# DeepFM forward pass on one core: later weight loads wait for the first gathered rows, the last tile's layer 1 outputs go by quarters, and the results are turned by VectorE in 32x32 blocks

## The chip, the core and the metric

The kernel runs on 1 core of one Trainium2 chip. The metric is the device time of one execution in microseconds (us). Three runs of the kernel before gave 155.88, 156.05 and 154.91 us, with a median of 155.88. One further execution was taken with the hardware profiler on. It took 154.75 us, of which its trace covers a span of 153.0 us.

## The reference

For 512 samples with 13 numeric and 26 categorical features the kernel computes a linear term, a factorization-machine term and a three-layer network, and adds them:

```
lin = bias + x_num @ w_num + lin_cat[fid, x_cat].sum(axis=1)
vn = x_num[:, :, None] * v_num[None, :, :]
vc = v_cat[fid, x_cat]                      # 26 rows of 64 numbers for each sample
v = concatenate([vn, vc], axis=1)
interactions = 0.5 * (v.sum(1)**2 - (v*v).sum(1)).sum(axis=1, keepdims=True)
deep_in = concatenate([x_num, vc.reshape(512, -1)], axis=1)      # 13 + 1664 columns
h = relu(deep_in @ W1 + b1)                 # 1024
h = relu(h @ W2 + b2)                       # 512
h = relu(h @ W3 + b3)                       # 256
return lin + interactions + h @ Wo + bo     # [512, 1]
```

All of it is in float32. The table holds 26 x 12500 rows of 65 numbers, the 64 of `v_cat` and the one of `lin_cat`.

## The kernel before

**Tiles and chunks.** The 512 samples are 4 tiles of 128 (one sample per partition, `t` = 0 to 3, `LAST` = 3). The 1664 gathered columns of a tile are 13 chunks of 128 columns (`c` = 0 to 12), two table rows each. So each chunk needs two indirect gathers, 26 for a tile and 104 in all. GpSimd (POOL) issues them in one row (lines 214 to 228). The buffer `g` holds 13 chunks, one tile: a gather for chunk `c` of the next tile waits until TensorE has turned that chunk, and until its squares and sums are done. `rows_in[c]` counts the gathers that have landed.

**Precision.** TensorE multiplies in fp32r. Each operand is therefore split in a high and a low part, and each product is three matmuls: high by high (L583), high by low weight (L590), low by high weight (L593). ScalarE makes high parts by a copy with rounding (`high_part`, `x_high`), VectorE makes low parts by a subtraction (`low_part`, `x_low`). For a weight's low part TensorE first copies the high part to PSUM (`twin`, L566).

**Weights.** 18 items of 128 x 1024 floats (512 KB each: 13 for W1, 4 for W2, 1 for W3) pass through a ring of 4 raw buffers. The loads are issued by SyncE (SP), in the order of lines 185 to 196; from the fifth on, each waits until the low part of the item four before is made (`lo_made`). In the same queue stand the categorical indices (`cat`), four copies of the numeric block (`hidden`, from which ScalarE and VectorE make `num_r` and the numeric terms), and `consts`.

**The order on TensorE is written out by hand.** A `step(t, c)` is `layer1_a` (L583), `turn_rows` of the next chunk (the transpose L574, which waits for that chunk's rows), and `layer1_b` (L590, L593). In tile 0 a `twin` stands before each step. Layers 2 and 3 of tile t-1 stand between the first steps of tile t. Engines run their instructions in order, so a wait in `turn_rows` holds all that follows it on TensorE.

**The results.** `interactions` (VectorE) gives `fm[:, t]`, `deep_sum` gives `deep[:, t]`, one number per partition. `result_row` (L700 to L706) turns both by a matmul against `ident` into one row of PSUM (two matmuls that add up), and VectorE copies that row to `out_row` (L449 to L451). For tiles 0 to 2 this stands inside a step of a later tile; for tile 3 it is the end of the program, followed by a store of 512 B.

**The last tile's end.** `layer1_last(3)` ends each half of layer 1 in its own PSUM bank. Then come relu by halves (L267 on ScalarE, L412 on VectorE), eight transposes of 128 columns (`turn_hidden1`, L642), high and low parts by halves (L271, L416), and layer 2 in two halves of 256 outputs (L792, L793, L798), then layer 3.

## Time and profile before

| | |
|---|---|
| three runs, median | 155.88 us (154.91 to 156.05) |
| profiled execution | 154.75 us |
| its span in the trace | 153.0 us |
| TensorE (PE) busy | 135.2 us, 88% of the span |
| GpSimd (POOL) busy | 99.6 us, 65% |
| VectorE (DVE) busy | 77.7 us, 51% |
| ScalarE (ACT) busy | 58.0 us, 38% |
| granted TensorE clock | 1.00 |

Each time is of one profiled execution. An engine's busy share is an average over the whole span: what an engine is worth at a certain place is read from what waits for it there. "issue" is time in which an engine waited for nothing that the profile shows. Line numbers (L225) are those of the kernel before.

### The profile page before, as it was taken

The page shows a single profiled execution, that of the slowest core. Times are in us where ns is not written, and L with a number is a line of the kernel's source. Part 1 is how long each engine was busy: PE and PEld are TensorE (multiplying, and loading weights), DVE is VectorE, ACT ScalarE, POOL GpSimd, SP SyncE. Part 2 cuts the span into 40 slices and gives each one's busy share as a digit, 9 for nine tenths or more (in the row PEclk, how much of TensorE's full clock was granted, in tenths as well). Part 3 has the DMA queues.
Part 4 walks back from the last instruction along what each step waited for, and adds up shares of the span by engine and source line. Part 5 has one row for each costly group of instructions (what it writes and reads, how often), then busy time and mean ns, then how long its engine had stood idle before and what let it go on. Part 6 is the DMA issues. An engine that isn't in the chain of part 4 may idle for free.

```text
span 153.0 us, 2072 instructions
## 1 busy us (share of the span) xinstructions
PE 135.2 (88%) x661; PEld 105.0 (69%) x661; DVE 77.7 (51%) x216; ACT 58.0 (38%) x153; POOL 99.6 (65%) x111
## 2 busy tenths in 40 slices
PE   0303999879999999999999999999999999999994
PEld 0102776547776676888767878778787887776992
DVE  4310587997699687232435524333446223353712
ACT  4501578666376631142333132223431423234120
POOL 3777777777777777777777777777777777700000
PEclk9999999999999999999999999999999999999999
DMA  4999677987777643343234343431344433310000
GB/s 107 372 123 311 103 208 197 298 261 198 192 232 201 175 27 29 28 29 25 27 25 33 26 26 28 27 31 27 25 30 27 30 28 25 28 9 4 0 0 0
DMA packets 6750, 13.66 MB, mean 89 GB/s; under 512 B 2578, under 2 KB 2708, under 8 KB 6740
## 3 DMA queue, kind: packets, MB, share of 16 engines
q0 software_dynamic: 3328, 3.47, 25.6%
q1 hardware_dynamic: 3412, 10.07, 21.0%
q8 instruction: 5, 0.08, 0.2%
q14 instruction: 5, 0.04, 0.1%
HBM read 13.53 MB, written 0.00 MB: 88 GB/s over the span
## 4 chain that ended last, share of the span: by engine, by line
PE 67%; DVE 13%; DMA 12%; issue 3%; ACT 2%; POOL 1%; DVEq 0%
PE acc L593 12%; PE acc L590 12%; PE acc L583 11%; DMA raw<-in_weights 6%; DMA g<-in_table,rows 6%; DVE w_lo L371 4%; PE acc L659 4%; PE acc L655 3%; PE acc L656 3%; PE xt_ps L574 3%; PE acc L677 2%; DVE num_r L376 1%; ACT w_hi L234 1%; DVE hidden L412 1%; PE ht_ps L566 1%
## 5 line engine op out<-in xcount | busy, mean ns | idle before, releaser
L225 POOL DMA_INDIRECT g<-in_table,rows x104 | 98.8, 950 | 33.2 <-issue 28.3
L398 DVE TENSOR_TENSOR x_lo<-xt_ps,x_hi 128x128 fp32r<-128x128 f32 x52 | 15.0, 288 | 50.0 <-ACT x_hi L241 50.0
L241 ACT ACTIVATE x_hi<-xt_ps 128x128 fp32r<-128x128 f32 x52 | 14.3, 275 | 68.6 <-PE xt_ps L574 68.4
L590 PE MATMUL acc<-w_lo,x_hi 128*128 128x512 f32 x96 | 34.8, 443 | 0.0
L583 PE MATMUL acc<-w_hi,x_hi 128*128 128x512 f32 x96 | 31.1, 405 | 0.8 <-ACT x_hi L241 0.5
L593 PE MATMUL acc<-w_hi,x_lo 128*128 128x512 f32 x96 | 30.8, 402 | 1.0 <-DVE x_lo L398 1.0
L593 PEld LDWEIGHTS acc<-w_hi,x_lo 128*128 128x128 f32 x96 | 18.1, 191 | 6.0 <-DVE x_lo L398 1.8
L583 PEld LDWEIGHTS acc<-w_hi,x_hi 128*128 128x128 f32 x96 | 17.7, 191 | 5.4 <-ACT x_hi L241 1.4
L234 ACT ACTIVATE w_hi<-raw 128x1024 fp32r<-128x1024 f32 x18 | 19.0, 1055 | 6.2 <-DMA raw<-in_weights 6.1
L574 PE MATMUL xt_ps<-ident,g 128*128 128x128 f32 x52 | 14.4, 278 | 6.8 <-DMA g<-in_table,rows 6.8
L590 PEld LDWEIGHTS acc<-w_lo,x_hi 128*128 128x128 f32 x96 | 14.7, 193 | 4.9 <-issue 0.9
L371 DVE TENSOR_TENSOR w_lo<-raw,ht_ps 128x512 fp32r<-128x512 f32 x24 | 15.8, 680 | 2.6 <-PE ht_ps L566 2.6
L404 DVE TENSOR_REDUCE field_sum<-g 128x64 f32<-128x256 f32 (+1 forms) x28 | 15.8, 563 | 0.0
L566 PE MATMUL ht_ps<-w_hi,ident_r 128*128 128x512 f32 x24 | 9.4, 433 | 6.1 <-ACT w_hi L234 6.1
L574 PEld LDWEIGHTS xt_ps<-ident,g 128*128 128x128 f32 x52 | 7.5, 144 | 9.9 <-DMA g<-in_table,rows 7.5
L251 ACT ACTIVATE junk_sq<-g 128x256 bf16<-128x256 f32 (+1 forms) x28 | 11.0, 393 | 0.1
L566 PEld LDWEIGHTS ht_ps<-w_hi,ident_r 128*128 128x128 f32 x24 | 5.0, 211 | 7.0 <-issue 6.1
L655 PE MATMUL acc<-w_hi,h1t_hi 128*128 128x512 f32 x24 | 9.6, 401 | 0.0
L656 PE MATMUL acc<-w_lo,h1t_hi 128*128 128x512 f32 x24 | 9.5, 396 | 0.0
L371 DVE TENSOR_TENSOR w_lo<-raw,acc 128x512 fp32r<-128x512 f32 x12 | 8.2, 680 | 2.4 <-PE acc L566 2.3
L659 PE MATMUL acc<-w_hi,h1t_lo 128*128 128x512 f32 x24 | 6.7, 400 | 0.1
L416 DVE TENSOR_TENSOR h1t_lo<-ht_ps,h1t_hi 128x512 fp32r<-128x512 f32 x8 | 5.4, 689 | 1.7 <-ACT h1t_hi L271 1.4
(99 smaller groups left out, 154.4 us busy)
## 6 DMA issues: line engine op xcount, KB each, us to landing
raw<-in_weights SPq DMA_DIRECT2D x18, 512.0 KB, 4.7
g<-in_table,rows POOLq DMA_INDIRECT x104, 3.4
hidden<-in_numeric SPq DMA_DIRECT2D x4, 108.1 KB, 7.0
consts<-in_row_consts SPq DMA_DIRECT2D x1, 129.0 KB, 9.2
cat<-in_x_cat SPq DMA_DIRECT2D x1, 39.0 KB, 4.3
cat<-in_x_cat SPq DMA_DIRECT2D x1, 13.0 KB, 1.7
out<-raw SPq DMA_DIRECT2D x1, 1.5 KB
out<-raw SPq DMA_DIRECT2D x1, 0.5 KB
```

What stands on the lines that cost most here:

```text
L225: pool.indirect_dma_start(g[:, c, a * ROW:(a + 1) * ROW], None, table, bass.IndirectOffsetOnAxis(rows[:, t, 2 * c + a:2 * c + a + 1], 0))\
L234: act.activation(w_hi[:, i, :], raw[:, i % RING, :], ACT.Copy).then_inc(hi_made, 1)
L241: act.activation(x_hi[:, n % SLOTS, :], xt(n), ACT.Copy).then_inc(xhi_done, 1)
L371: dve.tensor_tensor(w_lo[:, i, cols], raw[:, i % RING, cols], twin_ps[d % 3][:, :], ALU.subtract).then_inc(lo_made, 1)
L398: dve.tensor_tensor(x_lo[:, n % SLOTS, :], xt(n), x_hi[:, n % SLOTS, :].bitcast(F32), ALU.subtract).then_inc(xlo_done, 1)
L404: dve.tensor_reduce(field_sum[:, t % 2, j, 0:K], embeddings(j).rearrange("p c (a k) -> p k c a", a=2), AX.XY, ALU.add).then_inc(summed, 1)
L566: pe.matmul(twin_ps[d % 3][:, :], ident_r[:, :], w_hi[:, i, a * HALF:(a + 1) * HALF], start=True, stop=True).then_inc(twin_made, 1)
L574: pe.transpose(xt(n), g[:, c, 1:1 + P], ident[:, :]).then_inc(xt_done, 1)
L583: pe.matmul(acc[:, :], x_hi[:, n % SLOTS, :], w_hi[:, c, w], start=(c == 0), stop=False)
L590: pe.matmul(acc[:, :], x_hi[:, n % SLOTS, :], w_lo[:, c, w], start=False, stop=False)
L593: mm = pe.matmul(acc[:, :], x_lo[:, n % SLOTS, :], w_hi[:, c, w], start=False, stop=False)
L655: pe.matmul(acc2[:, :], h1t_hi[:, c, :], w_hi[:, i, w], start=False, stop=False)
```

## The change

It has three parts.

1. **Loads at the start.** SyncE issues `cat` of tile 0 and weights 0 and 1 as before, and then waits for the rows of chunk 0 before the rest of `cat` and weight 2, for those of chunk 1 before weight 3, and for those of chunk 2 before weights 4 and 5. The numeric copies follow in pairs around weight 6, `consts` follows weight 7. VectorE computes the row numbers of tile 0 before it zeroes `hidden`, and those of the other tiles only after the third chunk. The making of the numeric high and low parts and of the numeric terms moves some chunks later.
2. **Results.** `result_row` is gone from TensorE. VectorE adds `deep` and `fm` into a column of `result` (128 x 32), and transposes that tile in 32x32 blocks, once for tiles 0 to 2 and once for tile 3. A result then lies as four pieces of 32 numbers in four partitions. SyncE stores them with one DMA per tile, of 4 x 128 B.
3. **The last tile's layer 1 outputs by quarters.** Relu, transposes, high parts and low parts handle 256 columns at a time, in four PSUM banks, and TensorE starts layer 2 with the first quarter before the fourth is turned.

```diff
             sp.dma_start(cat[:, 0, :], x_cat[0:P, :]).then_inc(cat_in[0], 16)
             weight(0)
             weight(1)
+
+            chunk_landed(sp, 0, 0)
             sp.dma_start(cat[:, 1:TILES, :], by_tile[:, 1:TILES, :]).then_inc(cat_in[1], 16)
             weight(2)
+            chunk_landed(sp, 0, 1)
+            weight(3)
+            chunk_landed(sp, 0, 2)
+            weight(4)
+            weight(5)
             sp.wait_ge(num_zeroed, 1)
-            for k in range(P // STACK):
-                sp.dma_start(hidden[k * STACK:k * STACK + NROWS, :], numeric).then_inc(num_in, 16)
-            weight(3)
+            numeric_stacks(0, 2)
+            weight(6)
+            numeric_stacks(2, 4)
+            weight(7)
             sp.dma_start(consts[:, :], row_consts).then_inc(consts_in, 16)
-            for i in range(RING, ITEMS):
+            for i in range(8, ITEMS):
                 weight(i)
...
+            for t in range(LAST):
+                sp.dma_start(by_block[t], turned[t:P:STACK, 0, :]).then_inc(stored, 16)
+            sp.wait_ge(result_turned, 2)
+            sp.dma_start(by_block[LAST], turned[LAST:P:STACK, 1, :]).then_inc(stored, 16)
...
-                if c == 4:
+                if c == 7:
                     numeric_high()
-                if c == 7:
+                if c == 9:
                     numeric_squares()
...
-            hidden1_relu(LAST)
-            hidden1_high(LAST, 0)
-            hidden1_high(LAST, 1)
+            act.wait_ge(l1_half0, TILES)
+            for q in range(2):
+                act.activation(h1[:, quarter(q)], acc1[0][:, quarter(q)], ACT.Relu).then_inc(relu1a, 1)
+            for q in range(4):
+                act.wait_ge(h1t_done, 2 * LAST + q + 1)
+                act.activation(h1t_hi[:, 2 * q:2 * q + 2, :], quarter_ps[q][:, 0:QUARTER], ACT.Copy)\
+                   .then_inc(h1hi_done, 1)
...
-            def result_row(t, n):
-                dve.wait_ge(row_turned, t + 1)
-                dve.tensor_copy(out_row[:, t * P:(t + 1) * P], xt_rows(n)).then_inc(result_done, 1)
-
-            dve.memset(hidden[:, :], 0.0).then_inc(num_zeroed, 1)
+            def add_result(t):
+                dve.wait_ge(deep_done, t + 1)
+                dve.wait_ge(fm_done, t + 1)
+                dve.tensor_tensor(result[:, t:t + 1], deep[:, t:t + 1], fm[:, t:t + 1], ALU.add)\
+                   .then_inc(result_done, 1)
+
+            def turn_results(a):
+                dve.wait_ge(result_done, LAST + a)
+                dve.transpose(turned[:, a, :], result[:, :]).then_inc(result_turned, 1)
+
             dve.wait_ge(cat_in[0], 16)
             row_numbers(slice(0, FIELDS), 0)
-            dve.wait_ge(cat_in[1], 16)
-            row_numbers(slice(FIELDS, TILES * FIELDS), 2)
+            dve.memset(hidden[:, :], 0.0).then_inc(num_zeroed, 1)
...
-                if c == 5:
+                if c == 7:
                     dve.wait_ge(num_hi_made, 1)
                     numeric_low(slice(2 * STACK, P), slice(0, NX0))
-                if c == 6:
+                if c == 8:
                     numeric_low(slice(STACK, 2 * STACK), slice(NX0, NCOLS))
                     numeric_low(slice(2 * STACK, 3 * STACK), slice(NX0, NCOLS))
...
-                layer1_a(t, 7)
-                turn_rows(t, 8)
-                pe.wait_ge(xlo_done, t * CHUNKS + 8)
-                result_row(t - 1, t * CHUNKS + 7)
-                layer1_b(t, 7)
-
-                pe.wait_ge(result_done, t)
-                for c in range(8, CHUNKS - 1):
+                for c in range(6, CHUNKS - 1):
                     step(t, c)
                 layer1_last(t)
...
             pe.wait_ge(relu2, LAST)
             for acc, at in parts:
                 pe.matmul(acc, pick, num_r[:, at:at + QUARTER], start=True, stop=False)
+            pe.wait_ge(h2lo_done, LAST)
+            pe.wait_ge(relu1a, TILES)
+            turn_quarter(0)
+            pe.wait_ge(relu1a, TILES + 1)
+            turn_quarter(1)
+            pe.wait_ge(relu1b, TILES)
+            turn_quarter(2)
             pe.wait_ge(h1hi_done, 2 * LAST + 1)
             for acc, at in parts:
-                part2_high(range(0, 4), acc, at)
-            pe.wait_ge(h1lo_done, 2 * LAST + 1)
+                part2_high(range(0, 2), acc, at)
+            pe.wait_ge(relu1b, TILES + 1)
+            turn_quarter(3)
+            pe.wait_ge(h1hi_done, 2 * LAST + 2)
+            for acc, at in parts:
+                part2_high(range(2, 4), acc, at)
+            pe.wait_ge(h1lo_done, 2 * LAST + 2)
             for acc, at in parts:
                 part2_low(range(0, 4), acc, at)
...
-            result_row(LAST, 1)
```

**Order on SyncE at the start of the program.** Before, the queue has no wait ahead of the fourth weight but the one for `num_zeroed`:

```order
L185 DMA cat<-in_x_cat 128x26
L183 DMA raw<-in_weights 128x1024 x2
L188 DMA cat<-in_x_cat 128x3x26
L183 DMA raw<-in_weights 128x1024
L192 DMA hidden<-in_numeric 16x1730 [waits num_zeroed]
L192 DMA hidden<-in_numeric 16x1730 x3
L183 DMA raw<-in_weights 128x1024
L194 DMA consts<-in_row_consts 128x258
L183 DMA raw<-in_weights 128x1024 [waits lo_made] x14
```

In the changed kernel (its own line numbers) the same queue reads:

```order
L191 DMA cat<-in_x_cat 128x26
L185 DMA raw<-in_weights 128x1024 x2
L196 DMA cat<-in_x_cat 128x3x26 [waits rows_in0]
L185 DMA raw<-in_weights 128x1024
L185 DMA raw<-in_weights 128x1024 [waits rows_in1]
L185 DMA raw<-in_weights 128x1024 [waits lo_made,rows_in2]
L185 DMA raw<-in_weights 128x1024 [waits lo_made]
L189 DMA hidden<-in_numeric 16x1730 [waits num_zeroed]
L189 DMA hidden<-in_numeric 16x1730
L185 DMA raw<-in_weights 128x1024 [waits lo_made]
L189 DMA hidden<-in_numeric 16x1730 x2
```

The third weight now stands behind a wait for chunk 0's rows (`rows_in0`), and the numeric copies behind the sixth weight.

**Order on TensorE in the middle of tile 3.** Before, the step of chunk 7 holds the two matmuls of `result_row` for tile 2 (`fm`, `deep`), and the next step waits for `result_done`:

```order
L583 MATMUL acc1_1<-w_hi,x_hi 128x512
L574 MATMUL xt_ps1<-ident,g 128x128 [waits rows_in8,xlo_done]
L703 MATMUL xt_ps0<-ident,fm 1x128 [waits fm_done,xlo_done]
L705 MATMUL xt_ps0<-ident,deep 1x128 [waits deep_done]
L590 MATMUL acc1_0<-w_lo,x_hi 128x512
L590 MATMUL acc1_1<-w_lo,x_hi 128x512
L593 MATMUL acc1_0<-w_hi,x_lo 128x512 [waits xlo_done]
L593 MATMUL acc1_1<-w_hi,x_lo 128x512
L583 MATMUL acc1_0<-w_hi,x_hi 128x512 [waits xhi_done,result_done]
```

Now it is a plain step:

```order
L622 MATMUL acc1_1<-w_hi,x_hi 128x512
L613 MATMUL xt_ps1<-ident,g 128x128 [waits rows_in8,xlo_done]
L629 MATMUL acc1_0<-w_lo,x_hi 128x512
L629 MATMUL acc1_1<-w_lo,x_hi 128x512
L632 MATMUL acc1_0<-w_hi,x_lo 128x512 [waits xlo_done]
L632 MATMUL acc1_1<-w_hi,x_lo 128x512
L622 MATMUL acc1_0<-w_hi,x_hi 128x512 [waits xhi_done]
```

Two matmuls and two waits have gone from the row; the same holds for the results of tiles 0 and 1 in tiles 1 and 2.

**Order on TensorE behind layer 1 of the last tile.** Before, eight transposes of `hidden` stand ahead of the two bias matmuls (`num_r`) and of layer 2:

```order
L608 MATMUL acc1_1<-w_hi,x_lo 128x512
L642 MATMUL ht_ps0<-ident,hidden 128x128 [waits h2lo_done,relu1a]
L642 MATMUL ht_ps0<-ident,hidden 128x128 x3
L642 MATMUL ht_ps1<-ident,hidden 128x128 [waits h1lo_done,relu1b]
L642 MATMUL ht_ps1<-ident,hidden 128x128 x3
L804 MATMUL acc2<-num_r 128x256 [waits relu2]
L804 MATMUL xt_ps0<-num_r 128x256
L792 MATMUL acc2<-w_hi,h1t_hi 128x256 [waits h1hi_done]
```

Now the bias comes first, six transposes follow, and then layer 2's first quarter:

```order
L647 MATMUL acc1_1<-w_hi,x_lo 128x512
L823 MATMUL acc2<-num_r 128x256 [waits relu2]
L823 MATMUL xt_ps0<-num_r 128x256
L817 MATMUL ht_ps0<-ident,hidden 128x128 [waits relu1a,h2lo_done]
L817 MATMUL ht_ps0<-ident,hidden 128x128
L817 MATMUL ht_ps1<-ident,hidden 128x128 [waits relu1a]
L817 MATMUL ht_ps1<-ident,hidden 128x128
L817 MATMUL xt_ps1<-ident,hidden 128x128 [waits relu1b]
L817 MATMUL xt_ps1<-ident,hidden 128x128
L805 MATMUL acc2<-w_hi,h1t_hi 128x256 [waits h1hi_done]
```

The two transposes of the fourth quarter come eight layer 2 matmuls later.

## Rows read from the trace of the kernel before

**Rows 1.** Page: busy time, chain of waits, a costliest group, a DMA issue.

```profile
PE 135.2 (88%) x661; PEld 105.0 (69%) x661; DVE 77.7 (51%) x216; ACT 58.0 (38%) x153; POOL 99.6 (65%) x111
PE 67%; DVE 13%; DMA 12%; issue 3%; ACT 2%; POOL 1%; DVEq 0%
L225 POOL DMA_INDIRECT g<-in_table,rows x104 | 98.8, 950 | 33.2 <-issue 28.3
raw<-in_weights SPq DMA_DIRECT2D x18, 512.0 KB, 4.7
```

**Rows 2.** Timeline, GpSimd's gathers: start us, us, engine, line, operation [idle before].

```profile
3.43 1.10 POOL L225 DMA_INDIRECT g<-in_table,rows  x1 [1.77 <-DVE rows L365]
4.84 0.94 POOL L225 DMA_INDIRECT g<-in_table,rows  x1 [0.30 <-issue]
...
29.80 1.40 POOL L225 DMA_INDIRECT g<-in_table,rows  x1 [0.30 <-issue]
...
132.63 0.94 POOL L225 DMA_INDIRECT g<-in_table,rows  x1 [0.30 <-issue]
```

**Rows 3.** Line 225, issue to landing: second gather (4.84), last gather, all from 60 us.

```profile
DMA to landing us min/median/max: 9.2/9.2/9.2
...
DMA to landing us min/median/max: 3.6/3.6/3.6
...
DMA to landing us min/median/max: 2.4/3.3/3.6
```

**Rows 4.** Timeline, all engines, up to the first turned chunk.

```profile
1.17 1.50 DVE L453 MEMSET hidden<- 128x1730 f32 x1 [1.17 <-PEq L874]
1.37 0.29 POOL L211 TENSOR_SCALAR_AFFINE_SELECT ident<-ident 128x128 f32<-128x128 f32 x1 [0.16 <-POOL ident L209]
2.59 0.12 DVE L358 TENSOR_SCALAR wrap<-cat 128x26 f32<-128x26 int32 x1
...
14.12 0.47 PE L574 MATMUL xt_ps<-ident,g 128*128 128x128 f32 x1 [6.80 <-DMA g<-in_table,rows]
```

**Rows 5.** Timeline, VectorE's three subtractions with two SBUF sources.

```profile
29.08 1.29 DVE L376 TENSOR_TENSOR num_r<-hidden,num_r 64x1090 fp32r<-64x1090 f32 x1
...
31.92 1.68 DVE L376 TENSOR_TENSOR num_r<-hidden,num_r 32x640 fp32r<-32x640 f32 x2
```

**Rows 6.** Chain of waits in order of time: steps 7 to 9 of tile 3.

```profile
130.59 0.46 PE acc L583 x2
...
132.82 0.46 PE acc L583 x2
...
134.33 0.46 PE acc L583 x2
```

**Rows 7.** Timeline, the last transposed chunk and the end of layer 1.

```profile
137.65 0.27 PE L574 MATMUL xt_ps<-ident,g 128*128 128x128 f32 x1
...
139.87 0.39 PE L608 MATMUL acc<-w_hi,x_lo 128*128 128x512 f32 x1
140.25 1.45 PE L642 MATMUL ht_ps<-ident,hidden 128*128 128x128 f32 x8
...
141.78 0.28 PE L792 MATMUL acc<-w_hi,h1t_hi 128*128 128x256 f32 x1
```

**Rows 8.** Timeline, the end of the program.

```profile
150.61 0.08 DVE L445 DVE_READ_ACCUMULATOR junk_h<-acc,consts 128x1 f32 x1
...
151.16 0.28 DVE L451 COPY raw<-xt_ps 1x128 f32<-1x128 f32 x1 [0.47 <-PE xt_ps L705]
151.47 0.26 SPq L202 DMA_DIRECT2D out<-raw  x1
```

**Rows 9.** A stretch: PE, PEld, DVE, ACT, POOL busy, granted clock, DMA share, GB/s.

```profile
30.00:35.00 5.00, 4.01 (x18) 2.77 (x17) 4.88 (x9) 3.84 (x8) 4.03 (x4) 1.00 0.81 247
```

**Rows 10.** Timeline, pairs of matmuls in tile 0's first step and in tile 3.

```profile
15.25 1.05 PE L583 MATMUL acc<-w_hi,x_hi 128*128 128x512 f32 x2
...
134.17 0.62 PE L583 MATMUL acc<-w_hi,x_hi 128*128 128x512 f32 x2
```

More of the change, by code:

```diff
@@ L183, in weight, with numeric_stacks @@
                 sp.dma_start(raw[:, i % RING, :], weights[i]).then_inc(raw_in[i % RING], 16)
+            def numeric_stacks(k0, k1):
+                for k in range(k0, k1):
+                    sp.dma_start(hidden[k * STACK:k * STACK + NROWS, :], numeric).then_inc(num_in, 16)
             sp.dma_start(cat[:, 0, :], x_cat[0:P, :]).then_inc(cat_in[0], 16)
```

77 lines of the change are left out of this document (41 added, 36 removed).

## The prediction

> **What bounds the kernel now.** I read the page first. TensorE is busy for 135.2 us of the 153.0 us span and holds 67% of the chain of waits, so it looks like the bound, after a start that waits for DMA (12% of the chain) [rows 1]. The next view is the timeline at the start: TensorE turns its first chunk only at 14.12 us, after 6.80 us of idle time that the gather ends [rows 4]. The gather that it waited for was issued at 4.84 us and took 9.2 us to land, while gathers after 60 us need 2.4 to 3.6 us [rows 2, 3]. That is the delay at which the first part of the change aims, 9.2 less about 3.3, some 6 us.
>
> The view that decides is the timeline of GpSimd. It issues 104 gathers, each 0.94 us and then 0.30 us of "issue"; the busy sum of 98.8 us hides the second part [rows 1, 2]. The first starts at 3.43 and the last at 132.63 us: 129.2 us for 103 intervals, 1.254 us each, without a pause in which a buffer was missing. So GpSimd has no slack at all from 3.43 us on. The last gather lands at 132.63 + 3.6 = 136.23 us [rows 2, 3], and TensorE turns the chunk that it completes at 137.65 us [rows 7]. The whole work of TensorE before that place has therefore only 1.4 us of slack against the gathers. What TensorE gains beyond it, it spends waiting for rows.
>
> **The start, part by part.** *Gathers.* With weights 2 and 3, the numeric copies and `consts` held back, the second gather of chunk 0, issued at about 4.75 us, should land in 2.4 to 3.6 us, and somewhat later because weights 0 and 1 are still in flight: I take 8 us instead of 14. Tile 0 then runs at the pace of the gathers (2 x 1.254 = 2.5 us a chunk), and TensorE may be some 5 us ahead at its end. *Row numbers.* The zeroing of `hidden` (1.50 us) stood ahead of the row numbers, which start at 2.59 us [rows 4]. Now it stands behind them. When the indices land the trace does not show, as VectorE did not wait for them; the gain lies between 0 and 0.2 us, and I take **-0.1 us** for GpSimd's start, which moves every gather. *SyncE.* Behind its new waits stand weights 2 to 5; step c of tile 0 needs weight c+1, and each weight's load starts once chunk c-1's rows (c for weight c+2) are there. That costs TensorE waits in the first steps, but inside the 5 us. The numeric copies are issued later, and ScalarE's `numeric_high` waits for them at chunk 7 instead of 4, which at 2.5 us a chunk is room enough. All this I cost at nothing, and its cover is TensorE's new slack: a loss in tile 0 counts only once it is larger than the gain at the start plus the 2.2 us of the next item, less 1.4 us.
>
> *Result rows.* A step with `result_row` starts at 130.59 us and the next at 132.82, 2.23 us; a plain one takes 134.33 - 132.82 = 1.51 us [rows 6]. The change removes 0.72 us from each of three such steps, 2.16 us, all ahead of the last transpose. VectorE's row copy and its new addition are both small.
>
> *What of this counts.* TensorE would be ready for the last transpose at 137.65 - 2.16 - 5 = 130.5 us. The rows come at 136.23 - 0.1 = 136.13 us. The later one decides: the transpose starts at about 136.2 instead of 137.65 us, plus 0.1 us for a TensorE that starts from idle. I count **-1.35 us**, and not -7. Even with no gain at the start TensorE would be ready at 135.5, and the rows would decide all the same: if this is right, the first part of the change is worth nearly nothing by itself. Bounds: -2.5 if the last gather lands in 2.4 us, and 0 if the gathers slip by as much as they gain.
>
> **The last tile's end.** Before, layer 1 ends at 140.26 us, eight transposes run from 140.25 (1.45 us with a wait between), and layer 2 proper starts at 141.78 us [rows 7]. Now the two bias matmuls run at once, and ScalarE's first quarter is ready by then, since its whole half was. The transposes of quarters 0, 1 and 2 follow by 140.85, the first high part is there at about 141.2, and layer 2 starts at 141.2 instead of 141.78. It still has the two transposes of quarter 3 to do, some 0.27 us: **-0.3 us**. Bounds are 0 (more instructions, each with its fixed cost) and -0.6 (the last transposes free). Low parts and `interactions` run on VectorE behind this; `interactions` ends some 0.7 us later than before, and nothing needs it before the final addition.
>
> **The end of the program.** From the end of `deep_sum` (150.69 us) to the issue of the store (151.47) there are 0.78 us: a matmul of 0.38, a wait and a row copy of 0.28 [rows 8]. Now VectorE does an addition of one column and a transpose of 32 columns. The nearest rows are 0.12 us for 26 columns [rows 4] and 0.28 for the row copy of 128 [rows 8]. I take 0.15 for the addition and 0.2 for the transpose, with 0.08 of gaps, 0.43 in all: **-0.35 us**, bounds -0.5 and -0.1. The store is four pieces of 128 B instead of one of 512 B; I cost that at nothing, with up to +0.3 us in the range, since no row shows such a store.
>
> **The sum.** -0.1 - 1.35 - 0.3 - 0.35 = -2.1 us. On the profiled execution's 154.75 us this gives 152.65. The median of the runs lies 1.13 us above that execution, so the forecast for the median is 155.88 - 2.1 = **153.8 us**, 1.35% faster.
>
> **Rivals.**
>
> *The gather stream slips (chance 0.2).* One of the 104 gathers took 1.40 instead of 0.94 us. It was issued at 29.80 us, inside VectorE's subtraction with two SBUF sources, 29.08 to 30.37 [rows 2, 5]. The same line ran twice more, 31.92 to 33.60, and no gather was long beside those. Every such delay moves all later gathers and now stands fully in the time. The three subtractions now meet the gathers at other moments. If each is met and costs 0.3 to 1.2 us, the net loss is 0.5 to 2.1 us: 154.3 to 155.9 us. The Trainium skill (SBUF — State Buffer, section "SBUF: two separate sides") says that VectorE and GpSimd share a port pair as an exclusive lock, and that a GpSimd operation that reads SBUF is blocked by a VectorE operation with two SBUF inputs. By that rule each of the three would hold a gather that meets it; here one gather agrees, and beside the other two subtractions none was held. The zeroing of `hidden` I do not count, though it now stands beside the first gathers: beside it GpSimd's affine_select ran at 1.37 us in 0.29 us [rows 4].
>
> *TensorE stays the bound (0.08).* The gates starve the weights, and tile 0 ends later than before by more than 0.7 us. At 2 us later TensorE is ready at 137.5 us, and the gain is 0.15 + 0.65: 155.1 us. Against it speaks that a weight needs 4.7 us from issue to landing [rows 1] and four can be under way, so one could come every 1.2 us if nothing else waited.
>
> *The gathers do not bind (0.04).* If GpSimd's 1.254 us shrank with quieter DMA queues, TensorE's 7 us would show: 148 to 149 us. Against it: a gather takes GpSimd 0.94 us at 4.84 us, with the queues full, and at 132.63 us, with no load beside it [rows 2].
>
> *The clock falls (0.05), the one on the slow side.* In tile 3 TensorE now waits about 1 us at each of the last three chunks, and then runs layers 1 to 3 alone. In the first step after the long idle two matmuls took 1.05 us, later 0.62 [rows 10], a factor of 1.7. If the engine fell back so at the end, the 12.5 us from the last transpose to the end of layer 3 [rows 7, 8] would take some 9 us more: 162 us. It decides once those waits are long enough for the level to drop. Against it: at 30 to 35 us TensorE was busy for only 4.01 of 5 us, and the granted clock stayed at 1.00, the level of 2.4 GHz [rows 9]. The Trainium skill (TensorE: Matmul & The Clock Gate, section "HAM oscillation — how this bites in real kernels") warns that waits for DMA between batches of matmuls can throttle the clock again and again; no stretch of this trace shows it.
>
> **How the numbers follow.** My forecast has the remaining 0.63, with a range of its own of 152.8 to 154.7 us: the last landing, the end bounds, and runs that differ by 1.1 us among themselves. The full range reaches down to 152.4 and up to 155.8 us; about 2 in 10 stay out (clock, gathers that do not bind, the ends). About 1% is what a measurement of this kernel can tell from no change, 154.3 and 157.4 us. Faster: 0.7 of the forecast's 0.63, with 0.04 and some of the slip, makes 0.55 on paper, and I say 0.58 as the terms are one-sided. Slower: 0.07 (clock, and a slip with a store that costs more). The same: 0.35.
>
> **What would show it.** First transpose on TensorE at 7.5 to 9 us. GpSimd's gathers again 1.25 us apart, the last issued at 132.0 to 133.0 us. In tile 3 waits of TensorE for the rows of chunks 10, 11 and 12, some 3 us in all, where there were none; they are the proof that the gain at the start was given back. Last transpose at 136.0 to 136.6 us, from there to the end of the span 14.7 us instead of 15.35, layer 2 at 3.6 us behind the transpose (4.1 before), and 0.43 us between `deep_sum` and the store. Wrong is the forecast if TensorE meets no rows late in tile 3, or if a gather takes longer than 0.95 us in several places.

## The result, and the profile after

The change made the kernel slower: median 156.53 us (155.46 to 158.68, 20 runs) against 155.10 us (153.77 to 157.18, 20 runs) for the kernel before, a ratio of 1.0088 with a 95% interval of 1.0056 to 1.0120. Every ratio compares only the fast executions of the two kernels, those within 1.5% of the fastest, while a median is over all of them. The forecast of 153.8 us and its range, 152.4 to 155.8, are missed on the slow side. The profiled execution took 155.46 us, 0.7 more than that of before. It is the fastest of the 20 and the only one with a granted clock of 1.00, so the trace shows the change at its best.

The page after, the rows that answer to [rows 1], with the numeric copies added:

```profile
PE 134.9 (88%) x645; PEld 105.0 (68%) x645; DVE 78.8 (51%) x222; ACT 58.1 (38%) x156; POOL 99.9 (65%) x111
PE 69%; DMA 12%; DVE 11%; ACT 3%; issue 2%; POOL 1%; SPq 0%; DVEq 0%; ACTq 0%
L240 POOL DMA_INDIRECT g<-in_table,rows x104 | 99.1, 953 | 33.2 <-issue 30.2
L249 ACT ACTIVATE w_hi<-raw 128x1024 fp32r<-128x1024 f32 x18 | 19.0, 1055 | 17.1 <-DMA raw<-in_weights 17.1
L613 PE MATMUL xt_ps<-ident,g 128*128 128x128 f32 x52 | 14.6, 282 | 3.5 <-DMA g<-in_table,rows 3.5
hidden<-in_numeric SPq DMA_DIRECT2D x4, 108.1 KB, 8.6
```

The shares barely moved. What moved is line 249: ScalarE waited 17.1 us for weights to land, and this is the same row of the kernel before:

```profile
L234 ACT ACTIVATE w_hi<-raw 128x1024 fp32r<-128x1024 f32 x18 | 19.0, 1055 | 6.2 <-DMA raw<-in_weights 6.1
```

TensorE waited 3.5 us for rows (L613), in three places, all in the first 27 us. The timeline has the start and the last transpose (columns as in [rows 2]):

```profile
3.43 1.10 POOL L240 DMA_INDIRECT g<-in_table,rows  x1 [1.77 <-DVE rows L385]
4.84 0.94 POOL L240 DMA_INDIRECT g<-in_table,rows  x1 [0.30 <-issue]
...
8.14 0.47 PE L613 MATMUL xt_ps<-ident,g 128*128 128x128 f32 x1 [1.12 <-DMA g<-in_table,rows]
...
132.95 0.94 POOL L240 DMA_INDIRECT g<-in_table,rows  x1 [0.30 <-issue]
...
138.45 0.27 PE L613 MATMUL xt_ps<-ident,g 128*128 128x128 f32 x1
```

The first chunk is turned 6.0 us earlier than in [rows 4]; the last one 0.8 us later than in [rows 7], without an idle time in front of it: TensorE, not the gathers, sets it. In tile 3 TensorE waited for no rows at all, which the prediction had named as the sign that it is wrong. SyncE's issues in the first 23 us, and the stretches of the start (columns as in [rows 9]):

```profile
1.20 0.88 SPq L185 DMA_DIRECT2D raw<-in_weights  x2
8.11 0.39 SPq L196 DMA_DIRECT2D cat<-in_x_cat  x1
8.54 6.89 SPq L185 DMA_DIRECT2D raw<-in_weights  x4
15.48 0.89 SPq L189 DMA_DIRECT2D hidden<-in_numeric  x2
16.41 0.51 SPq L185 DMA_DIRECT2D raw<-in_weights  x1
16.97 1.12 SPq L189 DMA_DIRECT2D hidden<-in_numeric  x2
```
```profile
5.00:10.00 5.00, 3.05 (x7) 1.87 (x8) 2.33 (x5) 2.03 (x3) 3.78 (x5) 1.00 0.35 60
10.00:15.00 5.00, 3.68 (x9) 2.40 (x9) 1.34 (x4) 1.54 (x3) 3.78 (x5) 1.00 0.74 221
15.00:20.00 5.00, 4.46 (x16) 3.13 (x14) 3.43 (x10) 1.52 (x5) 3.78 (x5) 1.00 0.92 233
20.00:25.00 5.00, 2.91 (x12) 2.15 (x13) 2.64 (x7) 2.62 (x6) 3.78 (x5) 1.00 1.06 203
```

Read the last two columns. From 5 to 10 us the DMA engines move 60 GB/s; the kernel before had this there, and below it this from 20 to 25 us (TensorE's busy time is the second number):

```profile
5.00:10.00 5.00, 1.19 (x2) 0.50 (x2) 1.88 (x5) 2.04 (x2) 3.78 (x5) 1.00 1.11 243
20.00:25.00 5.00, 5.00 (x25) 3.96 (x24) 4.52 (x13) 3.42 (x8) 3.78 (x5) 1.00 0.71 178
```

(243 - 60) GB/s times 5 us is 0.9 MB less, nearly two weights of 0.5 MB. From 10 to 15 us the change moved 221 GB/s and the kernel before 267. From 15 us on it catches up, with full DMA engines (0.92 and 1.06), but at 20 to 25 us TensorE computes for 2.91 us and before for 5.00.

The long landings did not go away, they moved. The gathers issued in the first 8 us landed in 2.4 to 3.3 us (before 7.6 to 9.2). Those issued from 16 to 20 us took 7.9 to 9.2 us (before 3.7 to 4.5), and the weight issued at 16.41 us took 10.2.

### The profile page after: what moved, and what is told of

It reads as the page before. It is cut to its first block, busy times and chain, and to the rows that moved or that the text cites. A ratio compares the mean times of both kernels' runs of the same rounds, so it can differ in the third digit from the quotient of the medians.

```text
span 153.7 us, 2050 instructions
## 1 busy us (share of the span) xinstructions
PE 134.9 (88%) x645; PEld 105.0 (68%) x645; DVE 78.8 (51%) x222; ACT 58.1 (38%) x156; POOL 99.9 (65%) x111
## 3 DMA queue, kind: packets, MB, share of 16 engines
HBM read 13.53 MB, written 0.00 MB: 88 GB/s over the span
## 4 chain that ended last, share of the span: by engine, by line
PE 69%; DMA 12%; DVE 11%; ACT 3%; issue 2%; POOL 1%; SPq 0%; DVEq 0%; ACTq 0%
PE acc L622 12%; PE acc L632 12%; PE acc L629 12%; DMA raw<-in_weights 9%; PE acc L698 4%; DVE w_lo L391 4%; PE acc L694 3%; PE acc L695 3%; PE xt_ps L613 3%; DMA g<-in_table,rows 2%; PE ht_ps L605 2%; PE acc L716 1%; DVE num_r L396 1%; ACT w_hi L249 1%; PE acc L652 1%
## 5 line engine op out<-in xcount | busy, mean ns | idle before, releaser
L249 ACT ACTIVATE w_hi<-raw 128x1024 fp32r<-128x1024 f32 x18 | 19.0, 1055 | 17.1 <-DMA raw<-in_weights 17.1
L613 PE MATMUL xt_ps<-ident,g 128*128 128x128 f32 x52 | 14.6, 282 | 3.5 <-DMA g<-in_table,rows 3.5
L605 PE MATMUL ht_ps<-w_hi,ident_r 128*128 128x512 f32 x24 | 9.9, 453 | 7.2 <-ACT w_hi L249 7.2
L613 PEld LDWEIGHTS xt_ps<-ident,g 128*128 128x128 f32 x52 | 7.5, 144 | 7.5 <-issue 3.2
L605 PE MATMUL acc<-w_hi,ident_r 128*128 128x512 f32 x12 | 5.6, 463 | 1.7 <-ACT w_hi L249 1.7
(111 smaller groups left out, 151.9 us busy)
## 6 DMA issues: line engine op xcount, KB each, us to landing
consts<-in_row_consts SPq DMA_DIRECT2D x1, 129.0 KB, 10.2
```

The source lines that it names most:

```text
L249: act.activation(w_hi[:, i, :], raw[:, i % RING, :], ACT.Copy).then_inc(hi_made, 1)
L605: pe.matmul(twin_ps[d % 3][:, :], ident_r[:, :], w_hi[:, i, a * HALF:(a + 1) * HALF], start=True, stop=True).then_inc(twin_made, 1)
L613: pe.transpose(xt(n), g[:, c, 1:1 + P], ident[:, :]).then_inc(xt_done, 1)
```

## The experiments

The experiments are variants of the changed kernel, each with one thing taken back or altered; g1 to j2 are their names, and W0 to W17 the 18 weight items. Each transposed chunk starts a step, so the starts of a few transposes say where a kernel stands. "Copies" are the four numeric copies: *middle* is behind W5 and W6 as in the change, *early* ahead of the first gate or, without gates, behind W2 as before. "Places" are those of the numeric work on ScalarE, VectorE and TensorE: *late* as in the change, *old* as before. All kernels but the first have the results by VectorE, and all but the first and the one marked have the quarters. Times in us; all but the median are of one profiled execution. Kernels with the same start put tile 1 anywhere from 46.1 to 48.3 us, so a difference of 1 us there means little by itself.

| kernel | gates, copies, places | chunk 0 | chunk 4 | chunk 9 | tile 1 | last transpose | last gather | span | median |
|---|---|---|---|---|---|---|---|---|---|
| before | 0, early, old | 14.12 | 22.90 | 35.48 | 47.17 | 137.65 | 132.63 | 153.0 | 155.1 |
| the change | 3, middle, late | 8.14 | 23.29 | 36.64 | 50.49 | 138.45 | 132.95 | 153.7 | 156.53 |
| g1 start as before | 0, early, old | 13.06 | 21.89 | 34.47 | 46.10 | 136.38 | 132.91 | 151.6 | 153.57 |
| h8 the same, no quarters | 0, early, old | 13.53 | 22.58 | 35.72 | 47.45 | 136.44 | 132.97 | 151.9 | 153.90 |
| h3 no gates | 0, middle, late | 10.00 | 22.64 | 34.20 | 48.04 | 136.78 | 133.00 | 152.0 | 153.57 |
| h2 queue as before | 0, early, late | 10.93 | 21.97 | 33.94 | 47.80 | 136.27 | 132.80 | 151.5 | 153.65 |
| h5 numeric early | 3, early, late | 9.78 | 23.80 | 36.03 | 50.52 | 138.36 | 132.40 | 153.6 | 154.33 |
| i1 one gate | 1, middle, late | 8.28 | 23.12 | 35.96 | 49.91 | 137.83 | 132.56 | 153.1 | 155.11 |
| i2 gates alone | 3, early, old | 9.47 | 21.86 | 33.94 | 45.60 | 136.08 | 132.32 | 151.3 | 153.02 |
| j2 places back | 3, middle, old | 8.28 | 22.11 | 39.33 | 50.94 | 139.04 | 132.84 | 154.2 | 155.67 |
| j1 the change again | 3, middle, late | 8.23 | 25.64 | 39.46 | 53.31 | 141.30 | 133.29 | 156.5 | 156.71 |
| g7 queues never idle | 0, behind W2, old | 9.87 | 23.48 | 36.85 | 48.53 | 136.49 | 132.74 | 151.7 | 154.12 |
| i4 column pieces | 0, early, old | 10.77 | 22.91 | 35.20 | 46.88 | 135.79 | 132.33 | 151.0 | 153.44 |
| i3 stores of one piece | 0, early, old | 13.18 | 22.46 | 35.13 | 48.28 | 136.21 | 132.47 | 150.9 | 152.93 |

The kernel before ran beside each group, with medians of 154.84 to 155.39.

**A first series gave no answer.** Start as before (twice), queue as before, no gates and one gate (twice) ran first in conditions in which the kernel before took 217.3 and 208.5 us; TensorE, VectorE and ScalarE stopped together, for 5 to 19 us at a time. The kernels with one gate or none had ratios of 0.984 to 0.989 there; those with the start or the queue as before had medians of 217.2, 209.1 and 216.2 us, within 1.2 us of the kernel before. What stopped the engines is not shown, and no conclusion rests on these.

**The whole start taken back (g1).** SyncE's order, VectorE's zeroing ahead of the row numbers, and the places.

```diff
             weight(1)
-
-            chunk_landed(sp, 0, 0)
             sp.dma_start(cat[:, 1:TILES, :], by_tile[:, 1:TILES, :]).then_inc(cat_in[1], 16)
             weight(2)
-            chunk_landed(sp, 0, 1)
-            weight(3)
-            chunk_landed(sp, 0, 2)
-            weight(4)
-            weight(5)
             sp.wait_ge(num_zeroed, 1)
-            numeric_stacks(0, 2)
-            weight(6)
-            numeric_stacks(2, 4)
-            weight(7)
+            numeric_stacks(0, 4)
+            weight(3)
...
```

> The whole start is taken back (SyncE's order of issue, the order of VectorE's first operations, the places of the numeric work); the results by VectorE and the quarters stay. If the start is what made the change slower, the first transpose is back at 14.1 us, tile 1's first at 47.2, each later tile gains about 0.7 us on before from its removed result row, and the last transpose starts at about 135.5 to 136.5 us (bound then by the last gather's landing, 132.63 plus 3.6 = 136.2), with a span of about 151.5 to 152: some 1 to 1.5 us below the kernel before. If the start was harmless and something later (quarters, results, store) made it slower, this kernel is as slow as the changed one, span near 153.7.

Measured: 153.57 us, ratio 0.9921 (0.9892 to 0.9950), last transpose 136.38, span 151.6: the first theory, though chunk 0 and tile 1 come 1.1 us earlier than it said. The start cost the change 3.0 us of its median. Without it the rest gains 1.4 us on the kernel before; the prediction had 2.0 for these parts. The last gather was issued at 132.91, and its transpose waited for it.

**Gates, copies, places, one at a time.** No gates: the three `chunk_landed(sp, 0, ...)` lines are gone, nothing else.

> The changed kernel without its three waits on SyncE; the order of the loads (numeric copies behind W5 and W6) and the late places of the numeric work stay. If the queues that the gates leave idle cost the lead, the weights land as early as the queues allow, tile 1's first transpose comes at about 47.2 us as in the kernel before, or earlier, and the last one at about 136.2 to 136.4, where the rows bind; span about 151.6. If the place of the numeric copies or the late numeric work cost it, tile 1 still starts 2 to 3 us late, at 49.5 to 50.5, and the span stays near 153.7.

Measured: 153.57 us, ratio 0.9904 (0.9872 to 0.9936), span 152.0, tile 1 at 48.04: the first theory in time, though tile 1 starts 0.8 us later than it said and the last transpose, at 136.78, 0.4 us later.

Queue as before: SyncE's lines as in the diff above, all else as in the change.

> SyncE's order is that of the kernel before, without gates; on the engines the numeric work sits as late as in the changed kernel, and the other tiles' row numbers stay behind chunk 2. If the late numeric work costs time by itself, tile 1's first transpose comes 1 us or more behind 46.1 to 47.2 us; if it is harmless, it comes there and the kernel equals that with the whole start taken back: last transpose at 136.4, span 151.6.

Measured: 153.65 us, ratio 0.9938 (0.9903 to 0.9972). Tile 1 starts at 47.80, 1.7 us behind g1, and the span is 151.5: late places cost TensorE time, and the kernel nothing, since the rows bind at 136.27.

Numeric early: the gates stay, the copies move.

```diff
             weight(1)
+            sp.wait_ge(num_zeroed, 1)
+            numeric_stacks(0, 4)
...
             chunk_landed(sp, 0, 0)
...
-            sp.wait_ge(num_zeroed, 1)
-            numeric_stacks(0, 2)
             weight(6)
-            numeric_stacks(2, 4)
             weight(7)
```

> All three gates stay, but the four numeric copies go ahead of the first gate, where the queues would be idle at 5 to 10 us, and no longer into the middle of the weights. If the place of the numeric copies cost the lead, the weights W5 to W9 land in 5 us instead of 6.5 to 10, tile 1's first transpose comes back by 1.5 us or more, to 49 or earlier, and the span falls to about 152.3. If the missing megabyte of weights costs it, wherever the numeric copies stand, part of it comes back only as far as 0.43 MB is moved into the idle stretch: at 250 GB/s about 1.7 us of the 3.3.

Measured: median 154.33, ratio 0.9975 (0.9935 to 1.0015), 2.2 us below the change; but tile 1 in the profile at 50.52, as late as ever. Profile and median part here: the profiled execution took 155.37 us, 1.0 above the median. In the profile the granted clock fell behind the small matmuls of the numeric terms (66 columns and one, 42.5 to 44.6 us); it did not at that place in the change. That stretch of h5, then one step of h5 and the same of the change (chunk 12 of tile 0):

```profile
46.00:48.00 2.00, 2.00 (x7) 1.52 (x6) 1.89 (x7) 1.24 (x3) 1.49 (x2) 0.50 0.76 214
```
```profile
46.32 1.20 PE L628 MATMUL acc<-w_lo,x_hi 128*128 128x512 f32 x2
47.32 1.05 PE L631 MATMUL acc<-w_hi,x_lo 128*128 128x512 f32 x2
```
```profile
46.67 0.71 PE L629 MATMUL acc<-w_lo,x_hi 128*128 128x512 f32 x2
47.22 0.63 PE L632 MATMUL acc<-w_hi,x_lo 128*128 128x512 f32 x2
```

Chunk 12 to tile 1 took 4.27 us here and 3.85 in the change and h3; with the step before it, some 0.65 us of h5's tile 1 is the clock. The prediction of this run was wrong for the span and right for the direction.

Gates alone: the diff of h5, and the places as before, on three engines:

```diff
-                if c == 7:
+                if c == 4:
                     numeric_high()
-                if c == 9:
+                if c == 7:
                     numeric_squares()
...
-                if c == 7:
+                if c == 5:
                     dve.wait_ge(num_hi_made, 1)
...
-                if c == 10:
+                if c == 8:
                     numeric_terms()
+                if c == 9:
                     layer1_numeric(0)
```

> All three gates stay, the numeric copies go ahead of the first, and the numeric work on every engine sits where it sat before. Beside the kernel with the numeric copies early and the numeric work late (tile 1 at 50.5, span 153.6) it tells what the late places cost; beside that with the start taken back (46.1 to 47.5, 151.6) what the gates cost alone. If the gates are nearly all of it, tile 1 starts at 49.5 or later and the last transpose at 137.4 or later, span 152.7 to 153.6. If the late numeric work is half of it, tile 1 starts at 48.5 or earlier, the rows bind at 136.3 to 136.8 and the span is about 152.

Measured: 153.02 us, ratio 0.9850 (0.9808 to 0.9892), tile 1 at 45.60, span 151.3. The second theory, and more: the fastest complete kernel of all. So three gates do no harm to the time as long as the copies fill the idle queues and the numeric work sits early (with late places and the same queue, h5 took 154.33). It beats the kernel before by 1.5%; against g1 and i4 the 0.4 to 0.6 us are too few to be sure of.

Places back alone, gates and middle copies as in the change, and the change once more beside it:

> The changed kernel with all three gates and the numeric copies behind W5 and W6; only the places of the numeric work on ScalarE, VectorE and TensorE are those of before. In the profiles so far the late places add 1.2 to 1.7 us between chunk 4 and tile 1. If that holds here, tile 1's first transpose comes at 48.8 to 49.3 instead of 50.5, the last one at 136.8 to 137.3, the span at 152.1 to 152.7. If the copies, which landed at 24 to 26 us, come too late for the early places, ScalarE and VectorE wait there with the weights queued behind them and tile 1 starts at 50.5 or later, span 153.7 or more.

> The changed kernel, unaltered, on the same chip as the next one. A profile whose mean granted clock is below 1 shows where the clock falls. If a fall costs time only where TensorE binds, each stretch at the lower level, seen as pairs of matmuls at 1.05 to 1.20 us instead of 0.63 to 0.71, puts tile 1 later than 50.5 us by up to 1.7 us and the span goes up by the same. If the falls sit in stretches in which TensorE waits for weights, tile 1 stays at 50.5 and the higher median has another cause.

Measured: j2 155.67 us, ratio 1.0024 (0.9989 to 1.0060); j1 156.71, ratio 1.0085 (1.0043 to 1.0126), its profiled execution one of its longer ones. In both the clock fell. The stretches of j1, then of j2 (the granted clock is the third number from the end):

```profile
18.00:21.00 3.00, 0.43 (x2) 0.00 (x0) 0.88 (x2) 0.00 (x0) 2.24 (x3) 1.00 1.06 295
21.00:24.00 3.00, 1.62 (x4) 0.81 (x4) 1.39 (x3) 1.23 (x3) 2.23 (x3) 0.82 1.02 187
24.00:27.00 3.00, 1.36 (x4) 1.20 (x5) 1.05 (x4) 1.72 (x4) 2.39 (x3) 0.50 1.01 164
27.00:30.00 3.00, 3.00 (x9) 2.28 (x9) 1.28 (x2) 0.44 (x1) 2.09 (x4) 0.54 1.04 250
```
```profile
24.00:27.00 3.00, 0.78 (x3) 0.30 (x2) 1.49 (x3) 0.32 (x1) 2.39 (x3) 1.00 1.09 137
27.00:30.00 3.00, 1.65 (x5) 1.40 (x6) 0.00 (x0) 2.24 (x2) 2.08 (x4) 0.56 0.99 283
30.00:33.00 3.00, 3.00 (x9) 2.29 (x8) 2.30 (x6) 2.36 (x9) 2.39 (x3) 0.50 1.04 351
```

TensorE has computed for 0.43 of 3 us, or 0.78 of 3, and then runs at 0.50, the level of 1.2 GHz. The DMA share is at 1.0 all the while. In j1 TensorE waits there for a weight, in j2 for rows:

```profile
22.36 0.51 PE L605 MATMUL acc<-w_hi,ident_r 128*128 128x512 f32 x1 [3.92 <-ACT w_hi L249]
```
```profile
28.35 0.45 PE L613 MATMUL xt_ps<-ident,g 128*128 128x128 f32 x1 [3.57 <-DMA g<-in_table,rows]
```

j1's tile 1 at 53.31 is 2.8 us later than in the change and its span 2.8 longer: the first theory in kind, but more than its 1.7 us, since the waits were longer too. j2 has the numbers of its second theory (50.94 and 154.2) and only a part of its cause: its places cost 11.61 us from chunk 9 to tile 1, as everywhere, but chunk 4 to chunk 9 took 17.2 us, with the late rows and the fall, while `numeric_high` waited only 0.76 us for the copies. The medians say 1.0 us for the places.

One gate: the second and third `chunk_landed` on SyncE gone.

> Of the three waits on SyncE only the first stays, after it W2 to W5 are issued at once; the rest is the changed kernel. If any idle stretch of the queues costs its own length, the stretch from the landing of W1 (about 6 us) to the first gate's opening (8.1 us) stays and those behind it go: about 1 of the 2.5 us lost remains, tile 1's first transpose at 48.5 to 49.5, span 152 to 152.6. If the first gate costs nothing and the second and third all of it, tile 1 starts at 48.0 as without gates and the span is 152.0.

Measured: 155.11 us, ratio 0.9954 (0.9911 to 0.9997), tile 1 at 49.91, span 153.1. By the medians three gates against one cost 1.4 us, one against none 1.5; by the ratios it is 2.1 and 0.8, and the 0.8 is no larger than its uncertainty. With tile 1 1.9 us and the span 1.1 us behind h3, the first gate is most likely not free, but its share is not settled. The profile lies further to the slow side than the first theory had it, and does not fit the second.

**What bounds the faster kernels.** Never idle queues (g7): from W2 on a weight goes out when the one two before it has landed; row numbers first, old places, and the subtraction of 1,090 columns by two halves of its partitions.

```diff
+            def landed(i):
+                sp.wait_ge(raw_in[i % RING], 16 * (i // RING + 1))
...
+            for i in range(RING, ITEMS):
+                landed(i - 2)
+                weight(i)
```

> Row numbers first, and from W2 on each weight is issued when the one two before it has landed, so that never more than two are under way and never none; the numeric copies go behind W2, the numeric work sits where it sat before, and the 64-partition numeric subtraction is split into two of 32. If idle queues cost the change its lead, this kernel keeps most of it: first transpose at 8 to 10 us, tile 1's first well before 47.2 us, last transpose bound by the gathers at about 136.2, span 151.5 to 152. If the lead is lost whatever the queues do (TensorE's own work, the pace of the gathers, or weights that land no faster), tile 1 starts at 47 or later and the span is that of the kernel with the start of before, or longer.

Measured: 154.12 us, ratio 0.9957 (0.9928 to 0.9986), chunk 0 at 9.87, tile 1 at 48.53, last transpose 136.49, span 151.7. The lead of 4.2 us is gone by chunk 2 (18.62; before 18.94) although the queues are never idle. The second theory, then: the DMA engines are full from 5 to 15 us (shares of 0.95 and 1.01), and the early first chunk is not kept, here or in i2 (chunk 0 at 9.47, but chunk 4 at 21.86, against 21.89 in g1).

Column pieces (i4): g1 with the row numbers ahead of the zeroing, and

```diff
-                    numeric_low(slice(2 * STACK, P), slice(0, NX0))
+                    for a in range(0, NX0, 273):
+                        numeric_low(slice(2 * STACK, P), slice(a, min(a + 273, NX0)))
```

> SyncE's order and the places of the numeric work as before, the first tile's row numbers ahead of the memset and those of the others behind chunk 2 as in the change, and the numeric subtraction of 1,090 columns cut into four of 273 columns. If GpSimd's 104 gathers at 1.25 us are the bound now, an earlier first gather (3.31 instead of 3.43) and a gather that is held for at most one short piece (0.3 us instead of 0.6 to 0.8) bring the last gather to 132.3 to 132.6, the last transpose to 135.9 to 136.1 and the span to 151.1 to 151.4. If TensorE binds, the last transpose stays at 136.3 or later and the span at 151.5 or more.

Measured: 153.44 us, ratio 0.9877 (0.9837 to 0.9916), last gather 132.33, last transpose 135.79, span 151.0. The last transpose and the span are 0.1 us better than the first theory; the last gather came 0.58 us earlier than in g1 and the last transpose 0.59. The first gather was at 3.41 us, 3.43 in g1, so the gain is the shorter hold, 0.18 us against 0.68. That the pieces made it shorter is not shown: in i2 and i3 the whole subtraction held its gather for 0.24 and 0.06 us, because the gather began near its end. TensorE waited for the last rows in g1, h2, h3, h8 and i2 (0.3 to 1.2 us), and in i4 by some 0.2 us: there the gathers are the bound.

**The end.** Results alone (h8): g1 with the last tile's layer 1 outputs by halves.

> Start as before and the last tile's layer 1 outputs by halves as before; only the results are added and turned by VectorE. Beside the kernel with the start taken back it tells what the quarters are worth: by the profile of the changed kernel 0.2 to 0.3 us (its layer 2 ended 7.65 us behind the last transpose, 7.88 before), so a span 0.2 to 0.3 above that kernel's 151.6. If the quarters cost more TensorE time by their four small transposes and waits than they save, this kernel is as fast or faster.

Measured: 153.90 us, ratio 0.9944 (0.9908 to 0.9979), span 151.9: the quarters are worth 0.2 to 0.3 us, as expected (15.46 from the last transpose to the end of the span, with them 15.2).

One piece (i3): g1, and each store moves one piece of 128 bytes.

```diff
-                sp.dma_start(by_block[t], turned[t:P:STACK, 0, :]).then_inc(stored, 16)
+                sp.dma_start(by_block[t, 0:1], turned[t:t + 1, 0, :]).then_inc(stored, 16)
```

> The kernel with the start taken back, and each store moves only the first of its four pieces of 128 bytes (the other 96 results of each tile are not written). If the four pieces are what the end lost, the last issue falls from 0.50 us to 0.3 or less and from its start to the end of the span pass about 1.5 to 1.6 us instead of 1.97, so a span of 0.3 to 0.4 less than 151.6. If the loss lies in the larger number of stores or in the landing itself, issue to end stays at 1.9 to 2.0.

Measured: 152.93 us, ratio 0.9845 (0.9805 to 0.9886), span 150.9. The last issue, in i3 and then in g1:

```profile
149.49 0.23 SPq L209 DMA_DIRECT2D out<-turned  x1
```
```profile
149.69 0.50 SPq L209 DMA_DIRECT2D out<-turned  x1
```

From there to the end of the span 1.4 us against 1.9. Three more pieces cost 0.5 us, at the very end, where nothing hides them.

## Why the prediction failed, step by step

**The failed step** is "All this I cost at nothing, and its cover is TensorE's new slack". It held three things: the gates, the numeric copies between the weights, and the numeric work moved to later chunks. By the medians, with the other two as in the change, the gates cost 3.0 us (156.53 to 153.57), the place of the copies 2.2 (to 154.33), the late places 0.9 to 1.0 (156.71 to 155.67). They don't add: taken together they are 3.0 (g1). Without gates the late places are nearly free (153.65 against 153.57), and with early copies and old places the gates cost nothing (153.02, i2). It was the sum that passed the slack: tile 1 came 3.3 us late, and 1.2 were free.

*The slack was rightly priced, the lead was not.* In seven kernels that TensorE binds (the change, i1, h5, g7, j1, j2, i3) tile 1's first transpose and the last one are 87.8 to 88.1 us apart. The rows allow the last at about 136.3, so tile 1 may start at 48.3 and no later: the limit that the prediction gave, some 0.7 us later than before, came out at 1.2. But the lead of 5 us "at the end of tile 0" never was there. It was 6.0 us at chunk 0, 3.5 at chunk 2 (15.43 against 18.94), and gone at chunk 4 (23.29 against 22.90). The prediction divided 4.7 us a weight by four under way and got a weight every 1.2 us; that row is a median over the whole kernel. From 5 to 15 us the DMA engines were full, and a weight of 0.5 MB takes 2 us at the 243 to 267 GB/s they then moved. From chunk 2 to chunk 4 the kernel before already ran 1.98 us a chunk, with TensorE busy all the time. There was no faster pace to be had, and the 0.9 MB not moved while the gates were shut were made up only in part and too late: by the rates over the whole start, some 1.0 MB were missing at 15 us and 0.4 MB at 25 us. Weights and rows then queued together. g7 shows the other half: even without a gap the lead goes.

*The late places.* From chunk 9 to tile 1 all kernels with old places took 11.6 to 11.7 us (before, g1, h8, i2, i4, j2, g7; only i3, in whose profile the clock fell there, took 13.2), those with late places 13.8 to 14.0 (h5, with the fall, 14.5). In the change, then in g1, TensorE's waits and that stretch:

```profile
PE acc L632 <- DVE x_lo L418: 1.0, 1, 1.0
PE acc L647 <- DVE x_lo L418: 0.7, 1, 0.7
36.60:50.50 13.90, 12.24 (x56) 8.94 (x55) 11.35 (x27) 7.38 (x17) 10.60 (x11) 1.00 0.64 183
```
```profile
34.40:46.10 11.70, 11.70 (x55) 9.09 (x54) 9.39 (x25) 4.86 (x11) 8.96 (x10) 1.00 0.75 206
```

VectorE carries 2 us more in the late stretch (11.35 against 9.39), and TensorE waits 1.7 us for `x_lo`, once behind `numeric_low`, once behind `numeric_terms`. Chunks 4 to 9 give back some 0.6 us (h2 11.97, g1 12.58). The prediction only asked whether `numeric_high` would find its data, not what queues behind it. In the change the 3.3 us by which tile 1 is late are 0.4 at chunk 4, 0.8 more by chunk 9, and 2.2 more here.

*The clock.* The median rose by 1.4 us, the profile by 0.7. In the comparisons of g1 to j2 the kernel before had a mean granted clock of 0.99 or less in 30 of 97 executions, with a median near 156.0, and of 0.995 or more in the others, with 154.9: one fall, 1 us. The change had 1.00 in one of 20 executions (155.46 us), 0.985 to 0.989 in six (median 156.1) and less than 0.98 in 13 (median 156.9); in j1 it was below 0.98 in 9 of 12, in j2 in 8 of 12, in i1 in 7, in h5 in 4 and in h3 in 3. No execution of g1, g7, h2, h8, i2, i3 or i4 was below 0.98. So the fall was a rival for the right engine and the wrong end: not at the last chunks, where TensorE meets no rows, but in tile 0. The prediction had argued against it from one stretch in which TensorE computed for 4.01 of 5 us; ahead of the falls in j1 and j2 it stood nearly still. A wait is not the only thing ahead of a fall: in h5 and i3 TensorE was busy all the time and the fall came behind the small matmuls of the numeric terms. This is a pair of i3, 0.6 us behind the end of the last of them; the granted clock was 0.50 from 39 to 41 us:

```profile
38.92 1.05 PE L613 MATMUL acc<-w_hi,x_hi 128*128 128x512 f32 x2
```

Nor does each fall reach the span: in i2, the fastest complete kernel, the clock fell too, from 16 to 20 us, behind a wait of 2.1 us. The Trainium skill (TensorE: Matmul & The Clock Gate, "HAM oscillation — how this bites in real kernels") warned that waits for DMA between batches of matmuls can bring the clock down; j1 and j2 agree (0.43 and 0.78 of 3 us, then 0.50). That the missing 0.7 us is all clock is argued from these counts, not shown by a run; the waits that bring the clock down cost time themselves.

*What was right.* The first transpose at 7.5 to 9 us: 8.14. Gathers 1.25 us apart and the last at 132.0 to 133.0: 132.95. That the rows would bind at 136.0 to 136.6 if TensorE let them: 135.8 to 136.8 in six kernels (though the waits for rows in tile 3 were 0.2 to 1.9 us in all there, not some 3). And that "the first part of the change is worth nearly nothing by itself" even if it works: i2, with gates, against g1, 153.02 and 153.57 us. The result rows: the distance before was 90.48 us, now 88.0, so 2.5 us against 2.16 forecast; it went into the lateness of tile 1 instead of the span. The rival "TensorE stays the bound", with its gates that starve the weights, had the mechanism and 0.08 of the chance; it assumed a delay of 2 us, which gave 155.1, and the delay was 3.3.

*Small terms.* Row numbers first: -0.1 forecast, 0 measured in the change (3.43 again, after 1.77 us for the indices) and -0.1 to +0.1 in others with this order (3.31 to 3.57). Quarters: -0.3, measured -0.2 to -0.3. From `deep_sum` to the store 0.43 us forecast; these are the rows that answer to [rows 8], and the sum is 0.47:

```profile
151.18 0.08 DVE L465 DVE_READ_ACCUMULATOR junk_h<-acc,consts 128x1 f32 x1
151.30 0.16 DVE L472 TENSOR_TENSOR result<-deep,fm 128x1 f32<-128x1 f32 x1
151.49 0.21 DVE L477 STREAM_TRANSPOSE turned<-result 128x32 f32<-128x32 f32 x1
151.73 0.50 SPq L217 DMA_DIRECT2D out<-turned  x1
```

The store, costed at nothing with up to +0.3: +0.44 (1.97 from issue to end against 1.53), and i3 shows where it comes from. It ate the gain of the transpose. Layer 2 began 3.54 us behind the last transpose, forecast 3.6. From the last transpose to the end 15.25 us against 15.35 before; forecast was 14.7.

*The gather stream.* One gather was held again, for 1.73 us instead of 1.40, and the last gather was issued 0.32 us later than before (132.95 against 132.63). The rival was right in kind, with one hold instead of three; it cost nothing here, since TensorE was later still. See the last section.

## What to carry to other kernels

In this kernel a wait in front of a load was paid in bytes. For another, multiply the time that the queues will stand idle by the rate they moved in that stretch before, and ask which consumer misses these bytes, and when. Take the rate from that stretch's row, never from a median over the kernel. And when a step is moved, list what queues behind it on its own engine in the new place; "its data will be there" is not the price. Before one trace is taken for the kernel, look where its execution lies among the others: the change's was the fastest of 20.

## What the runs showed of the hardware

**What holds a gather.** The subtraction with two SBUF sources over 1,090 columns held the gather that began within it in 13 of the 14 profiles of the table (all but i1), and the gather then ended 0.82 to 0.83 us behind it, wherever it began. The change, g7 (two halves of 32 partitions, so two operations), and i4 (four pieces of columns):

```profile
35.66 1.29 DVE L396 TENSOR_TENSOR num_r<-hidden,num_r 64x1090 fp32r<-64x1090 f32 x1 [0.98 <-ACT num_r L271]
36.04 1.73 POOL L240 DMA_INDIRECT g<-in_table,rows  x1 [0.30 <-issue]
```
```profile
29.14 2.61 DVE L394 TENSOR_TENSOR num_r<-hidden,num_r 32x1090 fp32r<-32x1090 f32 x2
29.68 1.57 POOL L238 DMA_INDIRECT g<-in_table,rows  x1 [0.30 <-issue]
31.55 1.02 POOL L238 DMA_INDIRECT g<-in_table,rows  x1 [0.30 <-issue]
```
```profile
28.57 1.53 DVE L388 TENSOR_TENSOR num_r<-hidden,num_r 64x273 fp32r<-64x273 f32 x4
29.80 1.12 POOL L232 DMA_INDIRECT g<-in_table,rows  x1 [0.30 <-issue]
```

The end of the subtraction and 0.82 us give the end of the gather: 36.95 + 0.82 = 37.77; 31.75 + 0.82 = 32.57; 30.10 + 0.82 = 30.92. Halving the partitions spared nothing (holds of 0.63 and 0.08 us). With four short pieces the hold was 0.18 us, in g1 0.68; the whole subtraction gave 0.06 to 1.03 us, by where the gather began within it, so what the pieces take away is the long holds, and one profile does not show how much. In i1 the gather began at 34.99, with the subtraction (34.98), and was not held; the subtraction took 1.33 instead of 1.29 us. The 640-column pair held none in any profile, but there a gather began within 0.1 us of the place where the first of the two ends. The Trainium skill (SBUF — State Buffer, "SBUF: two separate sides") has it that whichever starts first keeps the shared port pair for its whole instruction; the held gathers fit it, i1's does not plainly, as it began 0.01 us behind the subtraction by the trace, and no run here separates this lock from another.

**The same start is not the same twice.** With the whole start as before (g1, h8, i3 and the kernel before) chunk 0 is turned at 13.06, 13.53, 13.18 and 14.12 us, and tile 1 starts at 46.1 to 48.3. The start is the same program in all four, so this is how far one execution and one chip differ from the next, 1.1 us at chunk 0 and, with i3's fall of the clock, 2.2 at tile 1. Little of it reaches the last transpose of g1, h8 and i3, which lies at 136.2 to 136.4. With SyncE's order of before but the row numbers ahead of the zeroing, chunk 0 came at 10.93 and 10.77 us (h2, i4): there the numeric copies are issued at 4.9 instead of 3.1 us, which may be why; no run varies this alone.
